# Second attention: score matmuls in pairs on two row tiles, with filler matmuls

## The chip, the core and the metric

The kernel is one program on one core of a Trainium2 chip. The metric is the device time of a whole execution in microseconds, the median of several runs.

## What is computed

The input is eight images of 256 x 256 and a text of 32 rows for each, together 288 tokens of 256 numbers for each image.

```python
def reference(x, txt, ...):
    h = tok(x)                          # wavelet split, gated details, synthesis
    h = concatenate([h, txt], axis=1)   # (8, 288, 256)
    h = h + L0_attn(layernorm(h))       # over the 8 images at one position
    h = h + L0_ffn(layernorm(h))        # 8 experts, top 2, and a shared one
    h = h + L1_attn(layernorm(h))       # the change is here
    h = h + L1_ffn(layernorm(h))        # 8 experts, top 2, and a shared one
    return h

def L1_attn(x, Wq, bq, Wk, bk, Wv, bv, Wo, bo):   # H, G, HD = 16, 4, 16
    q = (x @ Wq.T + bq).reshape(b, n, G, 4, HD)
    k = (x @ Wk.T + bk).reshape(b, n, G, HD)
    v = (x @ Wv.T + bv).reshape(b, n, G, HD)
    scores = einsum('bqghd,bkgd->bghqk', q, k) / sqrt(HD)
    y = einsum('bghqk,bkgd->bqghd', softmax(scores, -1), v).reshape(b, n, d)
    return y @ Wo.T + bo
```

So the second attention has, for each image, 16 query heads in 4 groups, each group with one key and one value head of 16 numbers.

## The kernel before, in words

The program holds the tokens in SBUF as `h`, 18 tiles of 128 rows (16 rows of each image in a tile). Six stages follow each other: the wavelet stage (to 52 us), the first attention (to 140), a layer norm with routing (to 159), the first experts (to 335), a layer norm and the second attention (to 611), and the output projection, routing and the second experts (to the end). Only the second attention changes.

Its numbers are float32 cut into a high and a low part (`split3` issues three matmuls for a product). For an image `i`:

- `project` makes q (two parts of 128 rows) and k, v (one part) for 288 positions, six matmuls for each of three parts `m`; DVE adds the bias (`qf`, L1135), ACT takes the high part (`qh`, L660), POOL the low part (`ql`, L457).
- SP writes `qh`, `ql` to DRAM (`stack_out`, L338) and reads them back (`stack_in`, L348, L351) as `QS` and `KS`: for each head the 16 numbers in rows 0 to 47, as high x high, high x low, low x high. Rows 48 to 95 are zero (`zeros`, L442). Rows 96 and 97 (`MROW`) hold the row maxima of the scores in `QS` and -1 in `KS`.
- Row scores (L1463, 36 for each image, 128 queries x 288 keys, banks 4 and 5 in turn) are made only for their maxima: DVE reduces each (L1125) into `MX`; after 18 of them PE transposes `MX` (L1510), DVE splits it into `Mh`, `Ml`, and SP sends it through DRAM into the rows 96 and 97 (`max_rows`, L358, L360).
- Transposed scores (L1481, 36 for each image, 96 keys x 384 queries, two at a time in banks 0 and 1 or 2 and 3) have K = 98: the product has the maximum taken off already. ACT takes the exponential of a pair of banks (L653) into the ring `PR`.
- Values (L1524): for each of 4 groups and 3 parts of keys, four matmuls, one for each head, into the four column tiles of bank 6. `VA` holds the values transposed (L1495) and a column of ones, which gives the sums. ACT copies each group out (`y_raw`, L707) and sends the sums through DRAM to be inverted and spread (L684 to L700; DVE L1148), and POOL multiplies (`divide`, L483, L486) into `yT`. The last image has its own way: PE spreads the sums (L1505), DVE inverts and multiplies (L1155 to L1163).

The work is one pipeline. `turn(it)` has `NU` = 18 steps `U`; turn `it` projects image `it`, makes the row scores of `it-1` (the first eight already in the turn before: `S_LEAD = 8`), the transposed scores of `it-2`, and the values of `it-2`, with the last in the turn of `it-3`. All engines run the same steps in the same order, written by the tables at the file's end:

```python
PR_U = [0, 1, 2]
VT_U = 3
MT_U = [5, 14]
SUM_U, SM_U, REC_U, RO_U, RB_U = [1, 2], 4, 7, 8, list(range(10, 18))
S_LEAD = 8
```

They give the steps of the projections, of the values' transposes, of the two transposes of the maxima, and of the sums' way. In one step PE issues two transposed scores, a row score, values if due, what the tables add, and a row score. Turns 4 to 7 are a loop. Behind the last turn come three `warm_up` matmuls and `out_project` (L1553).

Of the kernel before, what the change touches and what calls it, by code (L numbers as in the profile page):

```python
# [81 lines left out]
def build(nc, A, out):  # L82
# [156 lines left out]
    yr = [seq(f"yr{p}", [P, NGQ, POS], cur=k1) for p in range(2)]  # L239
# [3 lines left out]
    neg1 = at("neg1", [2, NGQ * POS], F32, k1[0])  # L243
# [60 lines left out]

    @block.sync
    def _(sp):
# [28 lines left out]
        def stack_out(i):

            sp.wait_ge(s["e_split"], 3 * (i + 1))
            sp.dma_start(scrH[ds(i, 1)].rearrange("o p m q -> (o p) m q"), qh[:, :, :].bitcast(F32)).then_inc(s["e_out"], 16)  # L338
            sp.dma_start(scrL[ds(i, 1)].rearrange("o p m q -> (o p) m q"), ql[:, :, :].bitcast(F32)).then_inc(s["e_out"], 16)

        def stack_in(i, p, m):

# [4 lines left out]
            for n, src in enumerate((scrH, scrH, scrL)):
                sp.dma_start(QS[p][n * HD:n * HD + HD, m * 8 * POS:(m + 1) * 8 * POS].bitcast(F32).rearrange("d (h q) -> d h q", h=8),  # L348
                             src[ds(i, 1), :, m, :].rearrange("o (h d) q -> d (o h) q", d=HD)).then_inc(s[f"e_in{m}"], 16)
            for n, src in enumerate((scrH, scrL, scrH)):  # L350
                sp.dma_start(KS[p][n * HD:n * HD + HD, m * 2 * POS:(m + 1) * 2 * POS].bitcast(F32).rearrange("d (g q) -> d g q", g=2),  # L351
                             src[ds(i, 1), m * 2 * HD:(m + 1) * 2 * HD, 2, :].rearrange("o (g d) q -> d (o g) q", d=HD)).then_inc(s[f"e_in{m}"], 16)

        def max_rows(i, p, b):
# [5 lines left out]
            sp.dma_start(QS[p][MROW:MROW + 2, b * NSH * P:(b + 1) * NSH * P].bitcast(F32),  # L360
                         scrM[ds(i, 1), :, b * NSH:(b + 1) * NSH].rearrange("o n c r -> (o n) (c r)")).then_inc(s[f"e_min{b}"], 16)

        def turn(it, p, pr, sp_, st):
            if pr:
                stack_out(it)
                if early(it):
                    stack_in(it, p, 0)
            if sp_:
                max_rows(it - 1, 1 - p, 0)
            if pr and not early(it):  # L370
                stack_in(it, p, 0)
            if sp_:
                max_rows(it - 1, 1 - p, 1)
            if pr:
                stack_in(it, p, 1)


        sp.wait_ge(s["e_const"], 3)
        turn(0, 0, True, False, False)
        sp.wait_ge(s["e_const"], 4)  # L380
        minus_ones(0)
        minus_ones(1)
        turn(1, 1, True, True, False)
        turn(2, 0, True, True, True)
        turn(3, 1, True, True, True)
        with sp.Fori(2, 4) as r:
            turn(2 * r, 0, True, True, True)
            turn(2 * r + 1, 1, True, True, True)
        turn(8, 0, False, True, True)
# [11 lines left out]
    def _(pool):  # L401
# [1314 lines left out]
```

## Time and profile before

| | |
|---|---|
| runs (3) | 848.50, 849.35, 849.79 us; median 849.35 |
| the profiled execution | 851.43 us, its span 849.6 us |
| granted TensorE clock, mean | 0.948 of 2.4 GHz |
| PE busy | 747.0 us (88%), 4842 matmuls |
| PEld (weight loads) | 632.8 us |
| DVE busy | 590.2 us (69%) |
| ACT busy | 340.3 us (40%) |
| POOL busy | 135.8 us (16%) |

The span goes from the first to the last instruction; the execution's own time is 1.8 us longer. PE is TensorE's matmuls and PEld its weight loads, which overlap them; DVE is VectorE, ACT is ScalarE, POOL is GpSimd, SP is SyncE, which issues DMAs. A granted clock of 1.00 is 2.4 GHz and 0.50 is 1.2 GHz. An engine's idle time matters only where it is on the way to the end.

### The profile page before, as it was taken

What the parts mean: (1) busy time and instruction counts of PE and PEld (TensorE: products, weight loads), DVE (VectorE), ACT (ScalarE), POOL (GpSimd) and SP (SyncE); (2) the same over time, 40 slices, a digit from 0 to 9 for tenths busy, and PEclk for the clock granted to TensorE, in tenths of its full rate; (3) what the DMA queues carried; (4) which work ended last, traced back from release to release, by engine and by line L of the source; (5) the groups of instructions that cost most, each with busy time, mean ns of one, the idle gap of its engine ahead of it and who ended that gap; (6) DMA issues with size and microseconds to landing.
All of it is one profiled execution on the core that took longest, in us unless ns stands there. A gap on an engine that the chain in (4) does not pass through costs nothing.

```text
span 849.6 us, 14457 instructions
## 1 busy us (share of the span) xinstructions
PE 747.0 (88%) x4842; PEld 632.8 (74%) x4842; DVE 590.2 (69%) x1357; ACT 340.3 (40%) x598; POOL 135.8 (16%) x128
## 2 busy tenths in 40 slices
PE   4639996899999998337999999999898999999997
PEld 3529994699999998226656556654476999999997
DVE  6295667677777777917676776773587777777776
ACT  1305443433333333200666666667434333333332
POOL 0105553000000000536113113311150000000000
PEclk9999996999999999556899999999999999999999
DMA  7210000000000000052434534430500000000000
GB/s 246 105 63 1 1 0 0 1 1 2 1 1 1 0 0 0 0 95 71 97 78 77 106 90 105 100 54 20 200 1 1 1 19 1 19 20 2 19 20 19
DMA packets 21559, 34.77 MB, mean 41 GB/s; under 512 B 6572, under 2 KB 17500, under 8 KB 20960
## 3 DMA queue, kind: packets, MB, share of 16 engines
q1 hardware_dynamic: 16632, 31.60, 13.9%
q10 hardware_dynamic: 4872, 2.46, 1.4%
q8 instruction: 32, 0.52, 0.3%
q14 instruction: 23, 0.19, 0.1%
HBM read 24.03 MB, written 9.99 MB: 40 GB/s over the span
## 4 chain that ended last, share of the span: by engine, by line
PE 78%; DVE 12%; ACT 3%; DMA 3%; issue 2%; SPq 1%; POOL 1%; ACTq 0%; DVEq 0%; POOLq 0%
PE PS L1222 17%; PE PS L1224 16%; PE PS L1223 16%; PE PS L1524 6%; PE PS L1463 6%; PE PS L1481 5%; DVE MX L1125 2%; PE PS L1553 2%; PE PS L1251 2%; PE PS L1230 1%; PE PS L1344 1%; PE PS L1310 1%; DMA KS<-scrH 1%; PE PS L1242 1%; DMA halves<-in_halves 1%
## 5 line engine op out<-in xcount | busy, mean ns | idle before, releaser
L1125 DVE TENSOR_REDUCE MX<-PS 128x1 f32<-128x288 f32 x288 | 125.1, 452 | 51.1 <-PE PS L1463 47.4
L1057 DVE SCALAR_TENSOR_TENSOR h<-PS,cmb,h 128x256 f32<-128x256 f32 (+1 forms) x342 | 143.9, 477 | 0.2 <-PE PS L1224 0.2
L653 ACT ACTIVATE PR<-PS 96x768 f32<-96x768 f32 x144 | 115.3, 806 | 47.3 <-PE PS L1481 44.9
L621 ACT ACTIVATE sg<-PS 128x384 f32<-128x384 f32 x114 | 55.8, 489 | 165.3 <-PE PS L1224 165.3
L1463 PE MATMUL PS<-KS,QS 96*128 96x288 f32 x288 | 97.9, 359 | 17.2 <-DMA KS<-scrH 14.9
L1042 DVE TENSOR_TENSOR al<-aa,ah 128x384 fp32r<-128x384 f32 x114 | 63.7, 558 | 67.0 <-ACT ah L625 67.0
L1463 PEld LDWEIGHTS PS<-KS,QS 96*128 96x128 f32 x288 | 57.2, 203 | 59.7 <-DVE MX L1125 40.3
L625 ACT ACTIVATE ah<-aa 128x384 fp32r<-128x384 f32 x114 | 59.9, 525 | 83.6 <-DVE aa L1036 83.6
L1222 PE MATMUL PS<-xTh,W1h 128*128 128x384 f32 x240 | 81.1, 338 | 0.0
L1036 DVE TENSOR_TENSOR aa<-sg,PS 128x384 f32<-128x384 f32 x114 | 63.3, 555 | 25.6 <-ACT sg L621 25.1
L1224 PE MATMUL PS<-xTl,W1h 128*128 128x384 f32 x240 | 80.9, 337 | 0.0
L1223 PE MATMUL PS<-xTh,W1l 128*128 128x384 f32 x240 | 80.9, 337 | 0.0
L1481 PE MATMUL PS<-QS,KS 128*96 128x384 f32 x288 | 75.7, 347 | 1.8 <-DVE MX L1125 1.0
L1222 PE MATMUL PS<-xTh,W0h 128*128 (+1 forms) x216 | 73.1, 338 | 0.0
L1224 PE MATMUL PS<-xTl,W0h 128*128 (+1 forms) x216 | 73.1, 338 | 0.0
L1223 PE MATMUL PS<-xTh,W0l 128*128 (+1 forms) x216 | 73.0, 338 | 0.0
L1524 PE MATMUL PS<-PR,VA 128*32 128x288 f32 x768 | 66.3, 418 | 1.1 <-ACT yr L707 1.0
L1222 PE MATMUL PS<-W1h,ah 128*128 128x256 f32 x180 | 51.1, 284 | 4.0 <-DVE al L1042 4.0
L1224 PE MATMUL PS<-W1l,ah 128*128 128x256 f32 x180 | 50.8, 282 | 0.0
L1223 PE MATMUL PS<-W1h,al 128*128 128x256 f32 x180 | 50.3, 279 | 0.0
L1222 PE MATMUL PS<-W0h,ah 128*128 128x256 f32 x162 | 46.0, 284 | 4.4 <-DVE al L1042 4.4
L1481 PEld LDWEIGHTS PS<-QS,KS 128*96 128x96 f32 x288 | 42.2, 165 | 9.5 <-ACT PR L653 4.5
(234 smaller groups left out, 1543.7 us busy)
## 6 DMA issues: line engine op xcount, KB each, us to landing
QS<-scrH SPq DMA_DIRECT2D x32, 144.0 KB, 3.8
W1raw<-in_w SPq DMA_DIRECT2D x1, 3840.0 KB, 11.5
W0raw<-in_w SPq DMA_DIRECT2D x1, 3456.0 KB, 10.6
scrH<-qh SPq DMA_DIRECT2D x8, 432.0 KB, 2.5
scrL<-ql SPq DMA_DIRECT2D x8, 432.0 KB, 3.2
QS<-scrL SPq DMA_DIRECT2D x16, 144.0 KB, 4.4
out_tokens<-h SPq DMA_DIRECT2D x6, 384.0 KB, 2.3
x_in<-in_x SPq DMA_DIRECT2D x2, 1024.0 KB, 6.5
```

What stands on the lines that cost most here:

```text
L625: A_(ah[:, b], aa[:, b], ACT.Copy).then_inc(s[f"f{L}_ah"], 1)
L653: A_(PR[0:KT, c0:c0 + 2, :], PS[0:KT, b:b + 2, 0:CW], ACT.Exp).then_inc(s["e_exp"], 1)
L1036: V.tensor_tensor(aa[:, b], sg[:, b], PS[:, 2 + b, 0:GW], ALU.mult).then_inc(s[f"f{L}_mul"], 1)
L1042: V.tensor_tensor(al[:, b], aa[:, b], ah[:, b].bitcast(F32), ALU.subtract).then_inc(s[f"f{L}_al"], 1)
L1057: ins = V.scalar_tensor_tensor(out=hj, in0=PS[:, b + t // 2, (t % 2) * D:(t % 2) * D + D], scalar=cmb[:, ds(g * GT + t, 1), e:e + 1].squee ...
L1125: V.tensor_reduce(MX[:, c // NSH, c % NSH:c % NSH + 1], PS[:, max_bank(it, c), 0:POS], AX_X, ALU.max).then_inc(s["e_mx"], 1)
L1222: M(out_, wh, xh, start=(start and c == 0), stop=False)
L1223: M(out_, wl, xh, start=False, stop=False)
L1224: ins = M(out_, wh, xl, start=False, stop=(stop and c == n - 1))
L1463: M(PS[:, max_bank(it, c), 0:POS], QS[q][0:MROW, c * P:c * P + P], KS[q][0:MROW, c // 9 * POS:c // 9 * POS + POS], start=True, stop=True). ...
L1481: ins = M(PS[0:KT, n % 4, 0:CW], KS[p][:, g * POS + kt * KT:g * POS + kt * KT + KT], QS[p][:, g * HQ + cc * CW:g * HQ + cc * CW + CW], sta ...
L1524: ins = M(PS[32 * hh:32 * hh + 32, 6, 0:POS], VA[p][:, kt, g, :], PR[:, c0:c0 + 3, :].rearrange("p c w -> p (c w)")[:, hh * POS:hh * POS + ...
```

## The change

- Scores in pairs. Heads of groups 0 and 1 now stand in rows 0 to 47 of `QS`/`KS`, those of groups 2 and 3 in rows 64 to 111, with the maxima in rows 48, 49 and 112, 113. Each step issues one pair of transposed scores (`scores`) and one pair of row scores (`row_scores`), the two of a pair on the row tiles at 0 and 64 and into two banks. Nothing is zero filled.
- DVE reduces both banks of a pair in one instruction. From turn 2 on all row-score pairs use banks 4 and 5, and each waits for the reduce before.
- `keep_busy`: two matmuls of 384 columns with no use, ahead of each projection (of images 2 to 7), values' transpose and maxima's transpose; and two at each step of turn 1 and of turn 2 up to step 8.
- Images 0 and 1 are projected ahead of the turns, then 16 `warm_up` matmuls; image `it+1` is projected in turn `it`. Row scores lag (`S_LEAD = -2`): image `it-1` from step 2 on, its last two in the next turn. Three buffers of `QS`, `KS` and `yr`. Values follow `AV_U`, in steps that have no projection; the second half of an image's values is in the next turn.
- The maxima's way is cut in two calls and has two reads; the inverses are read back a turn later (`RB_U`), those of image 6 in one piece behind turn 9. Half of image 0's stack is read by ACT's queue. The output bias is added in turns 3 to 5. No loops are left.

```diff
-MROW = 96
+TILE, MROW = 64, 48
-    QS = [seq(f"QS{p}", [P, NGQ * HQ], F32R, cur=k1) for p in range(2)]
+    QS = [seq(f"QS{p}", [P, NGQ // 2 * HQ], F32R, cur=k1) for p in range(NQB)]
...
+        for it in range(1, IMGS + 2):
+            if live(it, 0) and it > 1:
                 stack_out(it)
+            if live(it, 2):
+                max_out(it - 2, 1)
+                max_in(it - 2, 1)
+            if live(it, 0) and it > 1:
+                for a in range(2):
+                    stack_in(sp, it, a)
+            if live(it, 1):
+                max_out(it - 1, 0)
+                max_in(it - 1, 0)
...
+                if live(it, 4) and not last_image(it - 4) and U in RB_U and it < IMGS + 2:
+                    inverses_in(it - 4, RB_U.index(U))
+            if it == IMGS + 1:
+                for n in range(len(RB_U)):
+                    inverses_in(IMGS - 2, n)
...
-                    V.tensor_reduce(MX[:, c // NSH, c % NSH:c % NSH + 1], PS[:, max_bank(it, c), 0:POS], AX_X, ALU.max).then_inc(s["e_mx"], 1)
+                    V.tensor_reduce(MX[:, hf, z:z + NSH // 2 + 1:NSH // 2], PS[:, b:b + 2, 0:POS], AX_X, ALU.max).then_inc(s["e_mx"], 1)
...
+        def keep_busy(n, bank=6):
+
+            for _ in range(n):
+                M(PS[:, bank, 0:GW], xTh[:, 0, 0:P], xTh[:, 1, 0:GW], start=True, stop=True)
...
+        def scores(i, U):
+
+            g, kt, cc = U // 9, U % 9 // 3, U % 3
+            for a in range(2):
+                r = slice(TILE * a, TILE * a + MROW + 2)
+                ins = M(PS[0:KT, 2 * (U % 2) + a, 0:CW], KS[i % NQB][r, g * POS + kt * KT:g * POS + kt * KT + KT],
+                        QS[i % NQB][r, g * HQ + cc * CW:g * HQ + cc * CW + CW], start=True, stop=True, tile_position=(TILE * a, 0))
+            ins.then_inc(s["e_st"], 1)
+
+        def row_scores(i, c, bank):
+
+            g = c // (NSH // 2)
+            for a in range(2):
+                r = slice(TILE * a, TILE * a + MROW)
+                ins = M(PS[:, bank + a, 0:POS], QS[i % NQB][r, c * P:c * P + P], KS[i % NQB][r, g * POS:g * POS + POS],
+                        start=True, stop=True, tile_position=(TILE * a, 0))
+            ins.then_inc(s["e_s"], 1)
...
+                keep_busy(busy_at(it, U))
...
-                    wait(pe, s["e_mx"], NS * i + c - (3 if early(it) else 1))
+                    wait(pe, s["e_mx"], NSH * i + c - (1 if early(it) else 0))
+                    row_scores(i, c, max_bank(it, c))
...
+                if U in PR_U and live(it, -1) and it > 0:
+                    project(it + 1, PR_U.index(U))
...
+        for m in range(6):
+            project(m // 3, m % 3)
+        pe.wait_ge(s["e_prev"], 6)
+        warm_up(WARM)
+        last[0] = ("e_prev", 6)
+        for it in range(1, IMGS + 3):
+            turn(it)
...
-PR_U = [0, 1, 2]
-VT_U = 3
-MT_U = [5, 14]
+PR_U = [7, 12, 16]
+VT_U = 8
+MT_U = [11, 3]
-SUM_U, SM_U, REC_U, RO_U, RB_U = [1, 2], 4, 7, 8, list(range(10, 18))
+SUM_U, SM_U, REC_U, RO_U, RB_U = [9, 10], 14, 16, 17, list(range(4, 12))
-S_LEAD = 8
+S_LEAD = -2
+WARM = 16
+AV_U = [9, 10, 11, 13, 14, 15, 18, 19, 20, 22, 23, 24]
...
+def busy_at(it, U):
+
+    return 2 if it == 1 or (it == 2 and U < AV_U[0]) else 0
```

PE's order in the middle of turn 2 before: L1463 row scores, L1481 transposed scores, L1524 values, L1510 the transpose of the maxima.

```order
L1463 MATMUL PS<-KS_141,QS_139 128x288
L1524 MATMUL PS<-PR,VA_143 32x288 x4
L1463 MATMUL PS<-KS_141,QS_139 128x288
L1481 MATMUL PS<-QS_138,KS_140 96x384 x2
L1463 MATMUL PS<-KS_141,QS_139 128x288
L1524 MATMUL PS<-PR,VA_143 32x288 x4
L1463 MATMUL PS<-KS_141,QS_139 128x288
L1481 MATMUL PS<-QS_138,KS_140 96x384 x2
L1463 MATMUL PS<-KS_140,QS_138 128x288
L1510 MATMUL PS<-ident,MX 128x128
```

PE's order now, about steps 2 to 5 of a middle turn: L1452 a pair of transposed scores, L1461 a pair of row scores, L1477 values, L1428 fillers, L1533 the transpose of the maxima.

```order
L1461 MATMUL PS<-KS_142,QS_139 128x288 x2
L1477 MATMUL PS<-PR,VA_145 32x288 x4
L1452 MATMUL PS<-QS_138,KS_141 96x384 x2
L1461 MATMUL PS<-KS_142,QS_139 128x288 x2
L1428 MATMUL PS<-xTh 128x384 x2
L1533 MATMUL PS<-ident,MX 128x128
L1452 MATMUL PS<-QS_138,KS_141 96x384 x2
L1461 MATMUL PS<-KS_142,QS_139 128x288 x2
L1477 MATMUL PS<-PR,VA_145 32x288 x4
```

The number of score matmuls is the same; the row scores of a step stand together behind the transposed ones, and the fillers stand in a step without values.

ACT's order at the end of the turns before (L700 reads of the inverses of image 6, L653 exponentials, L707 copies of image 7's values):

```order
L700 DMA recb<-scrR 16x2x288
L653 ACTIVATE PR<-PS 96x768 [waits e_avt,e_st]
L707 ACTIVATE yr_154<-PS 128x288 [waits e_y,e_avt]
L700 DMA recb<-scrR 16x2x288
L653 ACTIVATE PR<-PS 96x768 [waits e_avt,e_st]
L700 DMA recb<-scrR 16x2x288
L653 ACTIVATE PR<-PS 96x768 [waits e_avt,e_st]
L700 DMA recb<-scrR 16x2x288
L707 ACTIVATE yr_154<-PS 128x288 [waits e_avt]
L718 ACT_TABLE_LOAD
```

And now (L666 exponentials, L684 the write of the inverses, L698 the reads, L704 the copies):

```order
L666 ACTIVATE PR<-PS 96x2x384 [waits e_st] x2
L684 DMA scrR<-rec 128x36 [waits e_rec]
L698 DMA recb<-scrR 16x2x288 [waits e_yt,e_ro]
L698 DMA recb<-scrR 16x2x288 x7
L704 ACTIVATE yr_156<-PS 128x288 [waits e_y,e_avt] x2
L715 ACT_TABLE_LOAD
```

The write and all eight reads of image 6 stand behind the last exponential and ahead of the last two copies.

## Rows read from the trace of the kernel before

**Rows 1.** The page, part 4: the chain that ended last, by engine.
```profile
PE 78%; DVE 12%; ACT 3%; DMA 3%; issue 2%; SPq 1%; POOL 1%; ACTq 0%; DVEq 0%; POOLq 0%
```
**Rows 2.** Stretch: length, busy us of PE, PEld, DVE, ACT, POOL, clock, DMA, GB/s.
```profile
456.00:482.00 26.00, 25.59 (x192) 15.44 (x191) 18.48 (x45) 17.04 (x29) 6.49 (x6) 1.00 0.45 94
```
**Rows 3.** Timeline of PE, transposed scores at turns' ends: start, length, instruction.
```profile
404.21 0.93 PE L1481 MATMUL PS<-QS,KS 128*96 128x384 f32 x2 [1.05 <-DVE MX L1125]
...
560.62 0.56 PE L1481 MATMUL PS<-QS,KS 128*96 128x384 f32 x2
...
582.49 0.95 PE L1481 MATMUL PS<-QS,KS 128*96 128x384 f32 x4
...
601.10 0.58 PE L1481 MATMUL PS<-QS,KS 128*96 128x384 f32 x2
```
**Rows 4.** Timeline of PE, one step with values.
```profile
497.93 0.51 PE L1481 MATMUL PS<-QS,KS 128*96 128x384 f32 x2
498.28 0.29 PE L1463 MATMUL PS<-KS,QS 96*128 96x288 f32 x1
498.50 0.69 PE L1524 MATMUL PS<-PR,VA 128*32 128x288 f32 x8
499.13 0.40 PE L1463 MATMUL PS<-KS,QS 96*128 96x288 f32 x1
499.37 0.51 PE L1481 MATMUL PS<-QS,KS 128*96 128x384 f32 x2
```
**Rows 5.** Timeline of PE, a projection's six matmuls; chain, six transposes.
```profile
510.11 0.40 PE L1222 MATMUL PS<-xTh,a1h 128*128 x1
...
511.03 0.30 PE L1463 MATMUL PS<-KS,QS 96*128 96x288 f32 x1
...
640.15 0.66 PE PS L1344 x6
```
**Rows 6.** Weight loads and matmuls of one L1524 group: ns min/median/max, first and last start.
```profile
L1524 PEld LDWEIGHTS PS<-PR,VA x8: 106/108/109, 498.5 to 498.6; 128*32 128x32 f32 x8
L1524 PE MATMUL PS<-PR,VA x8: 406/418/430, 498.5 to 498.8; 128*32 128x288 f32 x8
...
498.50 0.14 PEld L1524 LDWEIGHTS PS<-PR,VA 128*32 128x32 f32 x6 [0.21 <-issue]
```
**Rows 7.** DVE: reduces of row scores; the page's group; a reduce of 1152 elements.
```profile
499.57 1.89 DVE L1125 TENSOR_REDUCE MX<-PS 128x1 f32<-128x288 f32 x4 [0.50 <-PE PS L1463]
...
L1125 DVE TENSOR_REDUCE MX<-PS 128x1 f32<-128x288 f32 x288 | 125.1, 452 | 51.1 <-PE PS L1463 47.4
...
654.43 1.35 DVE L991 TENSOR_REDUCE t<-ra 128x144 f32<-128x1152 f32 x1
```
**Rows 8.** The page, part 5: ACT's exponentials.
```profile
L653 ACT ACTIVATE PR<-PS 96x768 f32<-96x768 f32 x144 | 115.3, 806 | 47.3 <-PE PS L1481 44.9
```
**Rows 9.** Head: PE's timeline, and stretches as in rows 2.
```profile
380.02 3.22 PE L1463 MATMUL PS<-KS,QS 96*128 96x288 f32 x9 [12.54 <-DMA KS<-scrH]
...
400.21 0.41 PE L1510 MATMUL PS<-ident,MX 128*128 128x128 f32 x1
...
381.00:382.00 1.00, 1.00 (x5) 0.68 (x3) 1.00 (x4) 0.00 (x0) 0.00 (x0) 0.50 1.03 110
...
388.00:392.00 4.00, 2.72 (x17) 2.04 (x15) 3.28 (x9) 0.89 (x4) 2.90 (x5) 0.96 0.19 75
...
396.00:400.00 4.00, 1.67 (x6) 1.12 (x5) 2.27 (x7) 0.00 (x0) 4.00 (x7) 0.50 0.69 85
```
**Rows 10.** Tail: DMA issues on ACT's queue, DVE's timeline, an issue group to landing.
```profile
595.74 0.83 ACTq L700 DMA_DIRECT2D recb<-scrR  x2
...
604.19 2.31 DVE L1158 SCALAR_TENSOR_TENSOR qf<-yr,halves,qf 128x288 f32<-128x288 f32 x1
...
610.40 0.46 DVE L1163 TENSOR_TENSOR yT<-qf,qf 128x288 f32<-128x288 f32 x1
...
scrR<-rec ACTq DMA_DIRECT2D x7, 18.0 KB, 2.1
```
**Rows 11.** Stretch in turn 9, columns as in rows 2.
```profile
594.00:597.00 3.00, 3.00 (x25) 1.44 (x24) 1.28 (x2) 2.38 (x4) 0.00 (x0) 1.00 0.09 25
```

More of the change, by code:

```diff
@@ L238, in build @@
     xn1 = at("xn1", [P, 2, GT, D], F32, k1[0])
[L239 removed]
+    yr = [seq(f"yr{p}", [P, NGQ, POS], cur=k1) for p in range(3)]
     SW = NGQ * HPG * POS // P
@@ L359, in max_rows, with max_in @@
+        def max_in(i, b):
             sp.wait_ge(s["e_mout"], 32 * (2 * i + b + 1))
[L360 to L364, printed above, removed]
-                stack_out(it)
[L366 to L375, printed above, removed]
@@ L378, in _ @@
[L378 to L389, printed above, removed]
+            for a in range(2):
+                r, c = TILE * a + MROW, b * NSH + a * (NSH // 2)
+                sp.dma_start(QS[i % NQB][r:r + 2, b * HQ:(b + 1) * HQ].bitcast(F32),
+                             scrM[i, :, c:c + NSH // 2].rearrange("n c r -> n (c r)")).then_inc(s[f"e_min{b}"], 16)
@@ L487, in divide @@
                                         recb[:, 2 * q + 1, :].rearrange("p (j c) -> p j c", j=NT), ALU.add).then_inc(s["e_yt"], 1)
[L489 to L498 removed]
+        for it in range(1, IMGS + 3):
+            if live(it, -1):
+                low_halves(it + 1)
+            if live(it, 4) and not last_image(it - 4):
+                divide(it - 4)
+            if 3 <= it < 6:
+                for j in range((it - 3) * NG, (it - 2) * NG):
+                    nc.gpsimd.tensor_tensor(h[:, j, :], h[:, j, :], bo1[:, :], ALU.add).then_inc(s["e_bo"], 1)
         pool.wait_ge(s["e_yl"], NGQ + 2)
@@ L717, in _ @@
+        for m in range(3):
+            high_part(0, m)
+        stack_in(act, 0, 1)
+        for m in range(3):
+            high_part(1, m)
+        for it in range(1, IMGS + 3):
+            turn(it)
         n1 = sum(WCOLS[1]) // NG
@@ L1531, in _ @@
         pe.wait_ge(s["e_hi"], NG)
-        for it in range(4):
-            turn(it, it % 2)
-        with pe.Fori(2, 4) as r:
-            last[0] = ("e_msplit", 2 * (2 * r - 1))
-            turn(2 * r, 0)
-            turn(2 * r + 1, 1)
-        last[0] = ("e_msplit", 14)
-        for it in range(8, 11):
-            turn(it, it % 2)
+        for m in range(6):
+            project(m // 3, m % 3)
+        pe.wait_ge(s["e_prev"], 6)
+        warm_up(WARM)
+        last[0] = ("e_prev", 6)
+        for it in range(1, IMGS + 3):
+            turn(it)
         warm_up(3)
```

386 lines of the change are left out of this document (185 added, 201 removed).

## The prediction

> **What bounds the kernel now.** I read the page's chain of waits first: 78% of it is TensorE (PE) [rows 1]. Then the stretches. In 456 to 482 us, the middle of the second attention, PE is busy 25.59 of 26 us at the full granted clock, DVE 18.48 and ACT 17.04 [rows 2]. So PE's own order sets the pace there. Then the timeline, for one step U (0 to 17 in a turn). Transposed scores (L1481) run from 404.21 (turn 2) over 560.62 (turn 8) and 582.9 (turn 9, the second pair of the four that begin at 582.49) to 601.10: six turns of 26.07, one of 22.3 with no projections and few row scores, and 18.2, 196.9 in all [rows 3]. All this is against the profiled execution, 851.43 us; the median of the runs is 849.35, that is 2.1 lower.
>
> One step with values, in PE's order [rows 4]: the scores L1481 at 497.93, the row score L1463 at 498.28, the values L1524 at 498.50, the next L1463 at 499.13, L1481 at 499.37. So two transposed scores take 0.35, values 0.62, a row score 0.22 ahead of values and 0.24 behind them, 1.43 in all. A matmul of 288 columns with no change of tiling ahead takes 0.137 (six of the projection from 510.11 to 511.03, less 0.10 for the change ahead of them [rows 5]). So a change into or out of column tiling costs about 0.10.
>
> **The change, part by part.**
> *Score pairs.* Per image 36 + 36 score matmuls of K = 98 and 96 become 18 + 18 pairs on two row tiles, 0-63 and 64-127. No row shows a row tile. The bounds: above, the pair costs as two (0.35 + 0.27); below, as one (0.175 + 0.137). The nearest rows are the column tiles of the values: eight weight loads of 108 ns each start within 50 ns [rows 6], and eight matmuls of 418 ns end 0.69 us after the first begins [rows 4]. Loads and matmuls of different tiles overlap there. I take the lower end and add 0.01 to 0.02 for the stagger.
> For each change between column tiles, row tiles and the whole array I charge the 0.10 that the rows show for column tiles.
>
> *The row-score loop.* Before, a row score waits for the maximum two back, in two banks. Now a pair fills both banks 4 and 5 and waits for the maximum of the pair just before it. One round: weight load to the start of DVE 0.44 (499.13 to 499.57 [rows 4, 7]); a reduce over 2 x 288 in place of 288, 0.45 + 288 x 1.04 ns = 0.75 (1152 elements take 1.35, 288 take 0.45 [rows 7], so 1.04 ns an element); release, by the gap between DVE's end and PE's start, 0.03. That is 1.22, and 1.33 if the second tile's load stands in line behind the first (0.11, the pitch of the transposes [rows 5]). PE's own work in a step with values: row pair up to the values 0.33 (its load is exposed), values 0.62, scores 0.28: 1.23. So the step takes 1.25, from 1.23 to 1.43 (nothing overlaps).
>
> *A full turn.* 11 steps with values at 1.25 = 13.75. Step 11 adds the maxima's transpose with its fillers (0.33 + 0.62 + 0.45 + 0.1 + 0.28): 1.77. The three projections: 0.33 + fillers (0.10 + 2 x 0.175) + six matmuls 0.82 + scores 0.28 = 1.88 each, 5.64. Step 8 (0.33 + 0.45 + three transposes 0.3 + 0.28) 1.35. Steps 3 and 17 at 1.25, the fillers of step 3 hidden in the loop. Waits for bank 7 at steps 8 and 12, 0.2. Sum 25.2. The twelve fillers are in it with 6 x 0.45 = 2.7, of which some 0.8 hides in the loop at steps 3 and 8. Without projections 23.3 (turns 7 and 8). Turn 9 is set by ACT: 18 x 0.80 for the exponentials [rows 8] and 4 x 0.41 for the copies = 16.1, I take 17.
> Turns 2 to 9: 5 x 25.2 + 2 x 23.3 + 17 = 189.6 against 196.9, **-7.3**.
>
> *Head.* The projections of both images now come first; image 0's end when they did, so its DMAs start when they did. Before, the first half of the stack releases PE at 380.02; now a pair needs both halves, and DMA is saturated to 382 (share 1.03 in its last microsecond [rows 9]). A second queue doesn't change the bytes, so 382. The zero fills of QS and KS go; they ended long before, so nothing. The larger fill of PR follows POOL's low halves of image 1; values need it some 25 us later, so nothing. What goes is the wait for image 1's stack, between 396 and 400, where PE is busy 1.67 of 4 us [rows 9]. Turn 1 is 16 steps: warm 0.77 each (fillers 0.45, pair 0.32), at 1.2 GHz about 1.4. With five at the low clock 7 + 8.5, three projections 3.6, transposes 1: 20. Turn 2 begins at 402 in place of 404.2: **-2**. Bounds: 399 (never cold) and 412 (all cold).
>
> *Tail.* ACT's order changes: the eight reads of image 6's inverses, which lay between exponentials, now stand ahead of image 7's last two copies of values. From the last scores T: the write of the inverses at T + 0.6, landed after 2.1, eight issues at 0.41 (two take 0.83) = 3.3, so the copy at T + 6 [rows 10]. Then three values 1.9, copy 0.5, and two chains of spread, reciprocal 1.96, product 0.52, sum 0.46, one after the other: the end at about T + 14.8, with one product stretched from 0.52 to 2.31, as at 604.19. Before: 610.86 - 601.10 = T + 9.8 [rows 3, 10]. **+5**. The second layer's weights are loaded once those reads have landed, 7 us ahead of the output projection where it was 7.4: nothing.
>
> *Queues and waits.* SP's order: the maxima's round trip. Before it took 4.0 us (transpose 400.21 to scores 404.21 [rows 3, 9]) and was given 13 steps; now it goes from step 11 to the next turn's step 0 and from step 3 to step 9, some 9.5 and 7.3 us, with two reads in place of one (+0.3) and, for the first half, some 2 us behind the stack's reads on SP's queue. It fits by 3 us, so nothing; if the reads of the inverses on ACT's queue slow it by more, PE waits (rival 3). POOL's additions of the bias move to turns 3 to 5, behind its low halves: nobody waits.
> Sum: -7.3 - 2 + 5 = -4.3: 847.1 profiled, **845.0** in the median.
>
> **The rivals.**
> 1. *The pair does not overlap, or row tiling drains longer than column tiling.* Then each step costs more. 104 steps (13 in each of seven turns, step 8, and three more in turns 7 and 8) carry it, so 10 ns a step is 1.04 us, and the point where the change turns slower is 41 ns a step. With the second load in line (1.33): -4.3 + 0.09 x 104 = +5, 854. With no overlap at all 11 steps at 1.43, 1.97, 3 x 2.08, 1.55, 2 x 1.37 and 0.2, a turn of 28.4: +3.2 in seven turns, 867. For it: no row tile in the trace; against: rows 6. The drain as a mechanism of this kernel: if each change had to wait for a matmul's flight beyond its own start, 0.30 - 0.14 = 0.16 [rows 5], in place of the 0.10 charged, twice a step, that is 0.12 x 104 = 12.5 us, 857.
> The Trainium skill (TensorEngine Tiling, Key Properties) has this as a rule: changing the tiling mode drains the engine. For column tiles the trace shows 0.10, less than the flight. The Trainium skill (TensorE: Matmul & The Clock Gate, Part 3) speaks for the overlap: matmuls on different row groups start some 4 ns apart; no row here shows it for row groups.
> 2. *The granted clock falls.* Before, turn 1 ran a row score (0.14 at the full clock) each 0.36 us: the clock, 0.96 at 388 to 392, was 0.50, which is 1.2 GHz, at 396 to 400 [rows 9]. In turn 9, where values and scores fill (12 x 0.62 + 18 x 0.35)/18.2 = three quarters, it stayed at 1.00, which is 2.4 GHz [rows 11]. A new step with values fills 0.62 + 0.18 + 0.14 of 1.25, three quarters too; steps 16 and 17 less. Each step at 1.2 GHz costs about 1 us. 2 of them a turn: +14, 859; one turn's worth in all, +18, 863.
> 3. *The maxima come late.* Each late half adds its lateness, once or twice a turn: 1 us each in seven turns is +14 at most, likely +5: 850.
> 4. *More gain:* the loop at 1.20, a warm turn 1, and a tail of +3: 839.
> 5. *It doesn't do what it says:* the built order shows pairs and fillers where they should be; whether the hardware overlaps them is rival 1.
>
> **How the numbers follow.** Forecast (overlap, clock up) 0.45, from 840 to 849; rival 4 0.10; rival 1 0.20 (the load in line 0.10, the drain 0.05, no overlap 0.05); rival 2 0.17; rival 3 0.08. The range takes in rival 4 and all but the ends of 1 and 2: 838 to 864. Within 0.2% (1.7 us, what a measurement can tell from no change) lie the upper edge of the forecast (0.05) and parts of rivals 1 and 3 (0.05): 0.10. Faster: 0.40 + 0.10 + 0.02 from rival 3 = 0.52. Slower 0.38.
>
> **What would show it.** Right: steps of 1.25 us, DVE's reduce on 576 elements at 0.75, PE waiting for it in steps with values; the pair's two matmuls starting within 0.03; turns of 25.2 and 23.3; first scores at 402; output projection some 15 us behind the last scores; clock 1.00 through turns 3 to 8. Wrong: pair matmuls 0.1 or more apart or the next step's start later than the reduce's end (rival 1), granted clock below 0.95 in turns 2 to 8 (rival 2), PE waiting for DMA QS<-scrM (rival 3).

## The result, and the profile after

The changed kernel takes 852.59 us in the median of 5 runs (850.86 to 854.15), the kernel before 849.35 (848.50 to 850.16). The ratio is 1.0039, 95% interval [1.0024, 1.0054]: **slower by 0.4%**, where 845.0 and "faster" were forecast. The intervals here leave out runs more than 1.5% above a kernel's fastest; where that matters below, all runs are given. The profiled execution of the change took 851.09 us (span 849.3), 0.3 less than the profiled one of before, 851.43; the balance below is made between these two.

One step with values, PE's timeline of the changed kernel (start, length, instruction), which answers to [rows 4]:

```profile
406.51 0.42 PE L1452 MATMUL PS<-QS,KS 50*96 50x384 f32 x2
406.82 0.40 PE L1461 MATMUL PS<-KS,QS 48*128 48x288 f32 x2
407.15 0.69 PE L1477 MATMUL PS<-PR,VA 128*32 128x288 f32 x8
407.77 0.41 PE L1452 MATMUL PS<-QS,KS 50*96 50x384 f32 x2
```

The step takes 1.26, and a pair of transposed scores 0.42 where two of them one behind the other took 0.51. The pairs overlap. DVE's group, from the page, which answers to [rows 7]:

```profile
L1128 DVE TENSOR_REDUCE MX<-PS 128x2 f32<-128x576 f32 x144 | 108.9, 757 | 68.8 <-PE PS L1461 67.6
```

The first transposed scores of turns 2 to 9 (step 0 of each), and the last (the lines between are left out), which answer to [rows 3]:

```profile
392.79 0.41 PE L1452 MATMUL PS<-QS,KS 50*96 50x384 f32 x2 [0.41 <-DVE MX L1128]
...
417.78 0.34 PE L1452 MATMUL PS<-QS,KS 50*96 50x384 f32 x2
...
443.35 0.33 PE L1452 MATMUL PS<-QS,KS 50*96 50x384 f32 x2
...
470.23 0.34 PE L1452 MATMUL PS<-QS,KS 50*96 50x384 f32 x2
...
496.01 0.34 PE L1452 MATMUL PS<-QS,KS 50*96 50x384 f32 x2
...
521.75 0.34 PE L1452 MATMUL PS<-QS,KS 50*96 50x384 f32 x2
...
545.20 0.34 PE L1452 MATMUL PS<-QS,KS 50*96 50x384 f32 x2
...
568.49 0.34 PE L1452 MATMUL PS<-QS,KS 50*96 50x384 f32 x2
...
594.05 0.76 PE L1452 MATMUL PS<-QS,KS 50*96 50x384 f32 x4
```

So the turns last 25.0, 25.6, 26.9, 25.8, 25.7 with projections, then 23.5, 23.3 and 25.9 (to the second of the last two pairs, 594.41): 201.6 against 196.9 before. The odd ones are the 26.9 and above all the 25.9 of turn 9, where 17 was forecast; there the granted clock is low. Stretches of the changed kernel (length, busy us of PE, PEld, DVE, ACT, POOL, clock, DMA, GB/s):

```profile
420.00:440.00 20.00, 19.57 (x165) 10.01 (x163) 12.52 (x20) 13.33 (x22) 1.60 (x2) 1.00 0.53 106
...
446.00:450.00 4.00, 4.00 (x27) 1.45 (x26) 1.58 (x3) 2.17 (x4) 3.55 (x6) 0.57 0.55 221
...
560.00:566.00 6.00, 5.31 (x47) 2.45 (x47) 3.67 (x7) 3.62 (x6) 3.75 (x3) 1.00 0.11 27
566.00:570.00 4.00, 2.64 (x22) 1.15 (x20) 2.56 (x4) 3.35 (x5) 0.44 (x1) 0.89 0.04 7
570.00:590.00 20.00, 19.32 (x113) 5.83 (x111) 2.08 (x4) 11.13 (x16) 1.02 (x1) 0.50 0.06 18
590.00:594.00 4.00, 4.00 (x26) 1.25 (x22) 2.33 (x2) 1.64 (x3) 3.16 (x3) 0.63 0.05 9
```

From 570 to 590 PE is busy 19.32 of 20 us and runs at 1.2 GHz all the while, where turn 9 of the kernel before stayed at 1.00 [rows 11]. Ahead of the two falls PE had pauses, in which it waited for the reduce of the maxima: it was busy 2.64 of 4 us from 566 on, and 3.15 of 4 from 442 on. A like stretch, 541 to 545 with 3.32 of 4, was followed by no fall. At the low clock a step of turn 9 looks like this, 1.68 instead of 0.9 to 1.0:

```profile
571.97 1.19 PE L1477 MATMUL PS<-PR,VA 128*32 128x288 f32 x8
573.09 0.63 PE L1452 MATMUL PS<-QS,KS 50*96 50x384 f32 x2
573.65 1.19 PE L1477 MATMUL PS<-PR,VA 128*32 128x288 f32 x8
```

The head went the other way. In the kernel before, DVE's small operations stood beside POOL's zero fills. POOL's timeline of the kernel before:

```profile
342.21 3.93 POOL L443 MEMSET QS<- 128x4608 f32 x1
346.09 1.05 POOL L444 MEMSET KS<- 128x1152 f32 x1
347.29 3.94 POOL L443 MEMSET QS<- 128x4608 f32 x1 [0.15 <-POOL KS L444]
```

DVE's of the same kernel:

```profile
342.40 4.77 DVE L748 TENSOR_SCALAR mv<-mt 128x3 f32<-128x3 f32 x1
...
347.42 3.83 DVE L753 TENSOR_SCALAR mt<-mv 128x3 f32<-128x3 f32 x1
```

and the same two operations in the changed kernel, where those fills are gone (L745 and L750 are L748 and L753 of before):

```profile
341.83 0.17 DVE L745 TENSOR_SCALAR mv<-mt 128x3 f32<-128x3 f32 x1
...
342.29 0.17 DVE L750 TENSOR_SCALAR mt<-mv 128x3 f32<-128x3 f32 x1
```

An operation on 128x3 elements took 4.77 us and ended at 347.17, when the fills of QS and KS end (346.09 + 1.05 = 347.14); the next took 3.83 and ended at 351.25, with the second fill of QS (347.29 + 3.94 = 351.23). This is what the Trainium skill (SBUF — State Buffer, Who interferes with whom) describes: GpSimd and some VectorE forms share a pair of ports, and the later one is blocked for the whole instruction. The chain of waits runs through these two operations, so the projections began at 362.82 before and at 354.27 now, 8.5 us earlier. From there to the first scores it is 38.5 us against 41.4: 2.9 more. The head gives 11.4.

The tail, in the changed kernel's chain of waits (start, length, what); it answers to [rows 10]:

```profile
594.87 1.46 DMA scrR<-rec
...
596.35 0.33 ACTq L698
600.10 0.42 ACT yr L704
...
603.14 1.97 DVE qf L1150
...
606.18 1.30 PE PS L1528 x2
607.47 3.27 PE PS L1223 x6
610.75 15.69 PE PS L1558 x72
```

The output projection (L1558) starts 16.3 us behind the last scores, 9.8 before: +6.5. Balance: -11.4 + 4.7 + 6.5 = -0.2, and the profiled executions differ by -0.3.

### The profile page after: what moved, and what is told of

Same layout as the page of the kernel before. It is cut to its first block, busy times and chain, and to the rows that moved or that the text cites. A ratio compares the mean times of both kernels' runs of the same rounds, so it can differ in the third digit from the quotient of the medians.

```text
span 849.3 us, 13715 instructions
## 1 busy us (share of the span) xinstructions
PE 762.6 (90%) x5012; PEld 619.7 (73%) x5012; DVE 566.2 (67%) x1213; ACT 341.0 (40%) x598; POOL 130.3 (15%) x124
## 4 chain that ended last, share of the span: by engine, by line
PE 81%; DVE 10%; DMA 2%; issue 2%; ACT 2%; SPq 1%; POOL 1%; ACTq 0%; DVEq 0%; POOLq 0%
PE PS L1215 16%; PE PS L1217 16%; PE PS L1216 16%; PE PS L1477 7%; PE PS L1452 5%; PE PS L1461 4%; PE PS L1428 4%; PE PS L1558 2%; PE PS L1244 2%; PE PS L1223 1%; PE PS L1337 1%; DVE MX L1128 1%; PE PS L1303 1%; PE PS L1235 1%; DMA KS<-scrH 1%
## 5 line engine op out<-in xcount | busy, mean ns | idle before, releaser
L1128 DVE TENSOR_REDUCE MX<-PS 128x2 f32<-128x576 f32 x144 | 108.9, 757 | 68.8 <-PE PS L1461 67.6
L666 ACT ACTIVATE PR<-PS 96x768 f32<-96x768 f32 x144 | 115.2, 806 | 62.8 <-PE PS L1452 62.1
L1033 DVE TENSOR_TENSOR aa<-sg,PS 128x384 f32<-128x384 f32 x114 | 63.2, 554 | 25.8 <-ACT sg L608 25.2
L1477 PE MATMUL PS<-PR,VA 128*32 128x288 f32 x768 | 73.7, 462 | 3.6 <-ACT yr L704 3.6
L1452 PEld LDWEIGHTS PS<-QS,KS 50*96 50x96 f32 x288 | 24.1, 165 | 55.5 <-issue 29.4
L1461 PE MATMUL PS<-KS,QS 48*128 48x288 f32 x288 | 54.5, 374 | 10.0 <-DVE MX L1128 9.5
L1452 PE MATMUL PS<-QS,KS 50*96 50x384 f32 x288 | 61.5, 428 | 1.1 <-ACT PR L666 0.7
L1461 PEld LDWEIGHTS PS<-KS,QS 48*128 48x128 f32 x288 | 27.7, 187 | 30.3 <-DVE MX L1128 15.0
```

The source lines that it names most:

```text
L666: A_(PR[0:KT, ca:cb + 1:cb - ca, :], PS[0:KT, b:b + 2, 0:CW], ACT.Exp).then_inc(s["e_exp"], 1)
L1033: V.tensor_tensor(aa[:, b], sg[:, b], PS[:, 2 + b, 0:GW], ALU.mult).then_inc(s[f"f{L}_mul"], 1)
L1128: V.tensor_reduce(MX[:, hf, z:z + NSH // 2 + 1:NSH // 2], PS[:, b:b + 2, 0:POS], AX_X, ALU.max).then_inc(s["e_mx"], 1)
L1452: ins = M(PS[0:KT, 2 * (U % 2) + a, 0:CW], KS[i % NQB][r, g * POS + kt * KT:g * POS + kt * KT + KT], QS[i % NQB][r, g * HQ + cc * CW:g * H ...
L1461: ins = M(PS[:, bank + a, 0:POS], QS[i % NQB][r, c * P:c * P + P], KS[i % NQB][r, g * POS:g * POS + POS], start=True, stop=True, tile_posi ...
L1477: ins = M(PS[32 * hh:32 * hh + 32, 6, 0:POS], VA[i % 2][:, kt, Y_G[n], :], PR[:, c0:c0 + 3, :].rearrange("p c w -> p (c w)")[:, hh * POS:h ...
```

## The experiments

The theory on record with the first seven: the clock falls because row-tiled pairs and column-tiled values hold it less than matmuls on the whole array; the zero fills slowed DVE; the tail is the eight issues on ACT.

**Without the fillers.** The two `keep_busy` calls at the transposes and the one in `project` go:

```diff
-                keep_busy(2, 7)
...
-                    keep_busy(2, 7)
...
-                    keep_busy(2, 7)
```

> The changed kernel without its 84 filler matmuls ahead of the projections and transposes. They are 12 of 0.22 us in a full turn, 2.6 us. Rival (fillers only cost): six full turns give back up to 2.6 each, 838 to 845. Theory (they hold the clock): the granted clock falls in turns 2 to 7 too, where a step with values takes 1.7 to 1.9 instead of 1.25; if half of the turns run so, 6 x 9 steps x 0.55 = 30 less 15, so 860 to 870.

Measured: 837.55 us (832.64 to 843.72, 6 runs), ratio to before 0.9844 [0.9820, 0.9868], 15.0 less than the changed kernel. **The rival was right**: the fillers only cost. (They have 384 columns and take 0.18 each at the full clock; the 512 columns and 0.22 of my expectations were wrong.) The transposed scores of step 17 in three turns with projections:

```profile
438.36 0.41 PE L1451 MATMUL PS<-QS,KS 50*96 50x384 f32 x2
...
462.33 0.41 PE L1451 MATMUL PS<-QS,KS 50*96 50x384 f32 x2
...
486.26 0.42 PE L1451 MATMUL PS<-QS,KS 50*96 50x384 f32 x2
```

24.0 a turn, 1.8 less than with fillers, and at the full clock. With 1.1 of turn 1 and the low stretch of turn 4 this kernel is 11.1 us ahead at the start of turn 7 (510.68 for 521.75); the rest of the 15.0 lies behind it, where the clock differs from run to run. The clock falls only from turn 7 on (stretches of this kernel):

```profile
456.00:482.00 26.00, 24.42 (x209) 12.17 (x209) 17.74 (x29) 17.94 (x30) 10.68 (x12) 1.00 0.59 105
520.00:540.00 20.00, 17.65 (x112) 7.02 (x108) 10.17 (x16) 11.26 (x19) 4.19 (x3) 0.60 0.49 72
540.00:560.00 20.00, 18.32 (x153) 7.37 (x145) 11.97 (x19) 12.46 (x21) 3.31 (x2) 0.89 0.09 22
```

From turn 7 on there are no projections. So my statement that fillers hold the clock in turns 2 to 7 falls for 2 to 6, and what the clock does in the last three turns is what sets the spread: the six runs go from 832.6 at a mean clock of 0.973 to 843.7 at 0.947.

**More fillers where it fell.** `keep_busy(more_at(it, U), 2 * (U % 2))` ahead of `scores`, with

```diff
+def more_at(it, U):
+    if it < 3:
+        return 0
+    return 2 if U == 17 or (it > IMGS - 2 and U in PR_U) or (it == IMGS + 1 and U in (MT_U[1], VT_U)) else 0
```

> The changed kernel with filler matmuls (full 128x128x512, two each time) also ahead of score pairs in stretches where the granted clock fell to 0.5 to 0.67 (446 to 450, 566 to 592): one place at the end of each turn from 3 on, three more in turns 7 to 9, two more in turn 9. Some 30 more fillers of 0.22 us are at most 7 us of TensorE time. Theory (the clock falls because the column-tiled value matmuls and row-tiled pairs do not hold it, and full-array matmuls do): the clock stays at 1.00 from 566 to 592, whose steps take 1.25 again instead of 1.7 to 1.9, some 10 us back after the fillers' own time, so about 842. Rival (fillers only cost time, the clock follows something else): the clock falls as before and the time is 855 to 860.

Measured: 845.06 us (844.42 to 860.57, 12 runs), ratio 0.9961 [0.9940, 0.9982]. As the theory had it: some 7.5 less than the changed kernel although PE has more to do. In the profiled execution the clock is 1.00 from 380 to 590. Ten of twelve runs lie between 844.4 and 847.9 with a clock of 0.966 to 0.975; two had a lower one (0.959 and 0.950) and took 854.6 and 860.6. The additional matmuls make the fall rarer; they don't exclude it. Whether they do it by their rows or by filling time is not shown: with them PE is busy 5.72 of 6 us from 566 to 572, where the changed kernel had the pauses, and the fillers on half of the rows, next, were not put at these places.

**Fillers on half of the rows**, same length and so the same busy share:

```diff
-                M(PS[:, bank, 0:GW], xTh[:, 0, 0:P], xTh[:, 1, 0:GW], start=True, stop=True)
+                M(PS[:, bank, 0:GW], xTh[0:TILE, 0, 0:P], xTh[0:TILE, 1, 0:GW], start=True, stop=True, tile_position=(0, 0))
```

(for bank 7 alone).

> The changed kernel with its fillers on 64 of the 128 rows (one row tile) and of the same length, so that TensorE's busy share is the same. Rival (the pauses of the engine decide about the clock): same time and same clock as the changed kernel, 852.6 within 2. Theory (matmuls on part of the array hold the clock less): the clock falls in more of the turns 2 to 7 and the time is at or above that without fillers, 860 to 880.

Measured: 852.88 us (850.90 to 858.40, 8 runs), clock 0.944 to 0.961. The median is the changed kernel's. The low clock begins one turn earlier in the profiled execution (0.66 at 540 to 566), but five of eight runs agree with the changed kernel's. This does not tell the two theories apart, and after the run without fillers one sees why: in turns 2 to 6 the fillers decide nothing.

**The rows of the scores, in the kernel before.** Its transposed scores run on all 128 rows (the `128*96` of [rows 4]), its row scores on 96, though only 50 and 48 of them carry data. Three kernels take rows away and leave the order, the number and the columns of the matmuls:

```diff
-MROW = 96
+MROW = 48
...
-        zeros(0)
-        zeros(1)
+        pool.sem_inc(s["e_const"], 2)
...
-                        ins = M(PS[0:KT, n % 4, 0:CW], KS[p][:, g * POS + kt * KT:g * POS + kt * KT + KT],
-                                QS[p][:, g * HQ + cc * CW:g * HQ + cc * CW + CW], start=True, stop=True)
+                        ins = M(PS[0:KT, n % 4, 0:CW], KS[p][0:MROW + 2, g * POS + kt * KT:g * POS + kt * KT + KT],
+                                QS[p][0:MROW + 2, g * HQ + cc * CW:g * HQ + cc * CW + CW], start=True, stop=True)
```

The two others have MROW = 66 and 62 and keep the zero fills.

> The kernel before, with its score matmuls on 50 rows instead of 98 and its row scores on 48 instead of 96, and therefore without the zero fills of QS and KS; no pairs side by side, no fillers. Theory for the start: the first projection comes at 354 instead of 362.8, 8.5 us of gain. Theory for the clock (matmuls on part of the array hold it less): the clock falls in more of turns 2 to 9 than before and takes some of the 8.5 back; if it does not, the time is 841.

> The kernel before with its transposed scores on 68 rows instead of 128 and its row scores on 66 instead of 96; zero fills kept, one matmul at a time as before, so only the number of rows differs from before, and no tile of 64 rows can be in play. Theory (the clock follows how much of the array the matmuls use): clock between the 0.82 of the version on 50 and 48 rows and the 0.95 of before, time between 870 and 940. Rival (a matmul of 64 rows or less is handled as a tile, and that makes the clock fall or the steps longer): clock and time as before, 850.

> The kernel before with its transposed scores on 64 rows and its row scores on 62, zero fills kept: only four rows fewer than the version on 68 and 66 (851.8, clock 0.942 to 0.949), fourteen more than the version on 50 and 48 (963, clock 0.79 to 0.83). If the clock follows the number of rows gradually: near the version on 68, 850 to 870. If what matters is whether a matmul reaches beyond 64 rows: near the version on 50, 930 to 975.

| rows, transposed / row scores | us, median (lowest to highest, runs) | clock, all runs |
|---|---|---|
| 128 / 96 (before, run beside each) | 848.8 to 850.4 (847.7 to 854.0) | 0.943 to 0.957 |
| 68 / 66 | 851.76 (849.87 to 854.87, 6) | 0.942 to 0.949 |
| 64 / 62 | 888.26 (874.74 to 915.15, 4) | 0.872 to 0.927 |
| 50 / 48 | 963.24 (945.67 to 975.48, 6) | 0.791 to 0.826 |

Stretches of the version on 50 and 48 rows, then of the one on 68 and 66, then of the one on 64 and 62:

```profile
400.00:440.00 40.00, 40.00 (x167) 23.27 (x168) 17.55 (x41) 16.49 (x27) 2.38 (x3) 0.50 0.17 40
440.00:460.00 20.00, 19.86 (x120) 11.90 (x119) 11.10 (x28) 10.32 (x19) 2.38 (x3) 0.80 0.37 88
...
476.00:482.00 6.00, 5.92 (x42) 3.55 (x40) 3.81 (x11) 4.00 (x9) 3.52 (x5) 1.00 0.23 86
482.00:500.00 18.00, 18.00 (x83) 9.48 (x82) 7.99 (x19) 7.91 (x11) 0.00 (x0) 0.50 0.30 66
```

```profile
503.00:520.00 17.00, 15.99 (x75) 9.66 (x74) 7.13 (x18) 6.05 (x10) 4.96 (x4) 0.60 0.29 48
520.00:560.00 40.00, 39.37 (x300) 23.73 (x298) 28.97 (x70) 27.12 (x46) 8.10 (x8) 1.00 0.46 100
```

```profile
440.00:457.00 17.00, 17.00 (x71) 10.36 (x72) 6.88 (x16) 5.69 (x8) 0.80 (x1) 0.50 0.22 36
...
480.00:560.00 80.00, 78.62 (x567) 46.23 (x564) 54.51 (x131) 50.11 (x84) 19.51 (x18) 1.00 0.42 90
```

On 50 and 48 rows PE is busy for 40 us without a pause and has 1.2 GHz, and at 482 the clock falls again though PE was busy 5.92 of the 6 us before. So here pauses of PE neither keep it low nor bring on this fall. Besides the rows only the zero fills were taken, and the version on 64 and 62 rows, which has them, loses the clock too. That rows matter in the kernel before is shown; by what law is not. The version on 64 and 62 shows something more: its clock stays low from the head of the attention to 457 and is 1.00 from there to the end of the scores, though the turns with projections are alike. So the same instructions ran for long at either level, and the four runs of this version spread over 40 us.

Of the expectations one had the size, the 850 that the rival gave for 68 and 66. On 50 and 48 rows the fall was to take back some of 8.5 us, and it cost over 110; the 888 on 64 and 62 lies between both forecasts. A time that follows the rows in proportion is excluded (128 to 68 costs 1.4 of 850, ratio 1.0014 [0.9993, 1.0034], and one low stretch in the profiled execution; 68 to 64 costs 36.5 in the medians). A mere boundary at 64 is not enough either, as 64 and 50 differ by 75.

The Trainium skill (TensorE: Matmul & The Clock Gate, Part 1) lets the clock depend on how busy the PE has been of late. Taken as the busy share of the profile, the trace of the version on 50 and 48 rows disagrees: 1.00 of busy time at a clock of 0.50.

The version on 50 rows also starts its projections at 353.83 instead of 362.82, 9.0 earlier, as expected without the fills.

**The fills put back** into the changed kernel, on POOL behind the fill of MX, with nobody using their result:

```diff
+        for p in (0, 1, 2, 0):
+            own(nc.gpsimd.memset(QS[p][:, :].bitcast(F32), 0.0))
+            own(nc.gpsimd.memset(KS[p][:, :].bitcast(F32), 0.0))
+            own.settle()
+        pool.sem_inc(s["e_const"], 1)
```

and the later waits for `e_const` one higher.

> The changed kernel with two zero fills of half-size QS and KS buffers twice over (the same 10 us of POOL's memsets as the kernel before has) put back behind the maxima's fill on POOL; nothing uses their result. Theory (POOL's fills stretched VectorE's small operations from 342 to 351): the first projection starts 8.5 us later again (362.8 instead of 354.3) and the time is about 861. Rival (the start came earlier for another reason, for example the order of waits): the first projection stays at 354 and the time at 852.6.

Measured: 859.62 us (857.26 to 864.25, 6 runs), ratio 1.0126 [1.0102, 1.0150], 7.0 more than the changed kernel; the first projection starts at 360.40, 6.1 later. The theory holds, with 6 to 7 in place of 8.5: these fills are half as long each and began 1.2 us earlier (341.02 for 342.21), and they met the two operations for 1.89 and 1.82 us instead of 4.77 and 3.83, and later three operations on 256 elements (3.77 for 1.05).

**The tail, with image 6's inverses on SP's queue**, alone and together with the additional fillers:

```diff
+        sp.wait_ge(s["e_ro"], 16 * (IMGS - 1))
+        sp.wait_ge(s["e_yt"], NGQ // 2 * (IMGS - 2))
+        for n in range(len(RB_U)):
+            hh, b = divmod(n, 2)
+            r = 32 * hh + HD * b
+            sp.dma_start(recb[r:r + HD, b::2, :], scrR[IMGS - 2, hh, b::2].unsqueeze(0).broadcast_to([HD, NGQ // 2, POS])).then_inc(s["e_rb"], 16)
...
-            if it == IMGS + 1:
-                for n in range(len(RB_U)):
-                    inverses_in(IMGS - 2, n)
```

> The changed kernel with the eight issues of image 6's inverses on SP's queue instead of ScalarE's, where they stood ahead of the copies of the last y. The trace of the changed kernel shows 3.65 us of them at 596.35 in the chain, and TensorE waiting 3.56 for the copy. Theory: 3.6 to 5 us less, 848 to 849. Rival (the end hangs on another chain that ends just as late, the division of image 6 on POOL): 851 to 853.

> The changed kernel with both the additional fillers and the last inverses on SP's queue. If the two losses are separate terms their gains add: about 842 less 4, so 838, which is faster than both kernels. If the additional fillers do nothing to the clock: 852 to 856.

Alone: 853.07 us (844.70 to 856.21, 12 runs), ratio 1.0013 [0.9987, 1.0039]; the clock went from 0.943 to 0.967 between its runs, and 11.5 us of spread hide a term of 4, so this run settles nothing. Together: 845.02 us (843.98 to 847.58, 5 runs), ratio 0.9934 [0.9915, 0.9953], against 845.06 with the fillers alone: **the gains don't add**. The two profiled executions show why. With both, the output projection starts at 603.74, 12.3 us behind the last scores, with the fillers alone at 607.02, 16.4 behind. (The clock has a part in this: from 596 to 605 it was low with the fillers alone and 1.00 with both.) What holds the output projection with both is the chain that the rival of the first of these two runs names, POOL's division of image 6: PE waits 2.28 for it. But the profiled spans are 845.8 and 845.6. DVE's timeline of the version with both:

```profile
619.58 0.96 DVE L1176 TENSOR_TENSOR h<-PS,h 128x768 f32<-128x768 f32 x1 [0.52 <-PE PS L1562]
620.57 1.08 DVE L837 BATCH_NORM_STATS2 stats<-h 128x6 f32<-128x256 f32 x3
621.69 0.23 DVE L744 TENSOR_TENSOR mt<-stats 128x18 f32<-128x18 f32 x1
621.84 2.92 DVE L745 TENSOR_TENSOR mt<-stats 128x18 f32<-128x18 f32 x1
624.68 0.18 DVE L746 TENSOR_TENSOR mt<-stats 128x18 f32<-128x18 f32 x1
```

and POOL's, the subtraction for the second layer's weights, which ends at 624.70:

```profile
613.20 11.50 POOL L498 TENSOR_TENSOR W1l<-W1raw,W1h 128x1280 fp32r<-128x1280 f32 x4 [9.52 <-ACT W1h L722]
```

An operation on 18 elements a row takes 2.92 and ends with POOL's. It is the same picture as with the zero fills. With fillers alone POOL is done at 622.97 and DVE comes to this place at 625: nothing collides. The weights' load waits for the reads of the inverses, so it came 1.1 us later (598.88 instead of 597.82), and 2.7 of the gain of 3.3 went in this one operation.

**Fillers only from turn 7 on**, with the tail on SP. The fillers of `project` go, those at the transposes stand under `FILL if it > IMGS - 2 else 0`, and

```diff
+def more_at(it, U):
+    if it < IMGS - 1:
+        return 0
+    return FILL if U == 17 or (it > IMGS - 2 and U in PR_U) or (it == IMGS + 1 and U in (MT_U[1], VT_U)) else 0
```

with FILL = 2, and then 1.

> The changed kernel with fillers only from turn 7 on, where no projections are left: two each at the additional places and at the transposes of turns 7 to 9; none in turns 2 to 6; the last inverses on SP's queue. Theory (in turns 2 to 6 the projections hold the clock and fillers only cost, from turn 7 on the clock falls without them): turns 2 to 6 take 23.9 as in the kernel without fillers, turns 7 to 9 keep 1.00 with 24.2, 24.5 and 19.0 as in the one with more fillers; 845.0 less 5 x 2.0, so 835. Rival (what holds the clock in turn 7 is the fillers of the turns ahead too): the clock falls in 6 or 7 as in the kernel without fillers, and the time is 838 to 845.

> The same with one filler at each place instead of two, 0.22 us less at some 17 places. If half as many full-array matmuls hold the clock: 835 less 3, so 832. If they don't: the clock falls in turns 7 to 9 in some runs and the time spreads from 832 to 842.

Measured with two: **835.69 us** (833.75 to 840.72, 5 runs), ratio 0.9828 [0.9801, 0.9855], 1.7% faster than before and 2.0% less than the changed kernel, and as the theory had it (835). Turns 2 to 6 take 23.3 to 24.0. Four of the five runs have a clock of 0.973 to 0.975 and take 833.8 to 836.2; the profiled one is the fifth, and lost some us:

```profile
535.00:550.00 15.00, 14.32 (x85) 5.30 (x84) 7.58 (x12) 7.33 (x10) 1.92 (x3) 0.57 0.06 12
```

With one: 842.75 us (830.53 to 850.65, 6 runs), two runs at 0.973 and 0.975 take 831.2 and 830.5, the four others, at 0.945 to 0.959, 842.7 to 850.7. One filler at each place is cheaper when the clock holds, and it held in two runs of six; so the second forecast, a spread, had the kind and not the size. Against the version with no fillers at all (837.55) the one with two is not told apart in the median; its runs spread over 7.0 us instead of 11.1.

## Why the prediction was wrong

**Score pairs and the loop: right.** "So the step takes 1.25": 1.26 measured, the reduce 757 ns for 0.75. In steps without values PE waits 0.68 for the reduce and the step is 1.25 as well; in those with values the weight load of the row pair starts 0.05 behind the reduce's end (408.07 for 408.02). So the loop sets both, as forecast. Rival 1 is out, the pair overlaps and changes of tiling cost no more than charged.

**Full turns: nearly.** "Sum 25.2": 25.6 to 25.8 at the full clock (the 26.9 has the low stretch at 446 to 450 in it), 25.0 in turn 2. The fillers' share, 2.7 less 0.8 hidden a turn, was right: taking them out gave 1.8. What I did not ask is whether anything was won by them there. Turns 7 and 8 took 23.5 and 23.3 where I had 23.3 for each. The five turns with projections are 129.0, forecast 126.0, and 1.2 of that is the clock: this part of the sum held to 2 us.

**Granted clock: the step that failed.** The forecast set turn 9 at 17, at the full clock. It took 25.9, nearly all of it at 1.2 GHz. In the version with both, at 1.00 from 560 to 600, turn 9 took 19.3 with 12 additional fillers of 0.18 in it, so some 17.1 without, which is an estimate. So the low clock cost about 25.9 - 17.1 = 8.8, and 1.2 more in turn 4 (26.9 for 25.7): **some 10 us** of the 12.0 by which turns 2 to 9 exceed the forecast. In the tail it cost 1.7 (1.19 for 0.69 in the last values, 1.27 and 1.30 for 0.68 in two spreads), where the kernel before had lost 0.5 in one spread (1.16). Rival 2 had the mechanism ("the granted clock falls", 0.17) and near enough the size (+14), but looked at steps 16 and 17 of full turns; it happened above all in turn 9, and there I had argued from how much of the time matmuls *fill* (three quarters before, three quarters after). The runs on fewer rows show that this quantity does not decide alone: with the same matmuls in number, order and columns the mean clock was 0.95 on 128 and 96 rows and 0.79 to 0.83 on 50 and 48. The text also gave the scores "K = 98"; the row says `128*96`, all rows of the array, and I read past it. What is shown is that the clock fell in turn 9, what it cost, and that additional matmuls there mostly bring it back. That the pairs lose it by their rows, as the kernel before does when its rows are taken, is argued and not shown; the pauses ahead of the fall are a rival that no run separates from it.

**Head: a second step that failed, by 9 us in the other direction.** "The zero fills of QS and KS ... ended long before, so nothing." They ended before their readers, and that was the wrong question. The chain of waits of before had the two operations of 4.77 and 3.83 us on 3 elements a row in it, and I did not look at that stretch. Even the rows had a case of it: the product stretched "from 0.52 to 2.31, as at 604.19" stood beside POOL's division (603.59 to 606.20), and in the changed kernel it took 0.91. Putting fills back costs 7.0. This also moved the row scores' start from 382 to 373.5. The rest of the head, "2", was 2.9: turn 1 never went cold and took 19.3 from the first row scores, for which I had 20.

**Tail: right in kind.** +5 forecast, +6.5 measured; the 1.7 of the low clock are in it. The terms as I named them give more than the T + 14.8 that I wrote: 6 + 1.9 + 0.5, twice 2.94, and 1.8 for the stretch are 16.1. Against that the 16.3 measured is near partly by luck, as the stretch was 0.4 and the low clock made up for it. "The second layer's weights ...: nothing" holds for the change, but they stand just behind it: when the tail was shortened by 3.3, DVE's wait behind POOL's subtraction of these weights took 2.7 of it.

**Maxima and queues: right.** PE waits nowhere for QS<-scrM. Rival 3 is out.

So the profiled -0.2 is -8.5 (fills, missed), -2.9 (rest of the head), +4.7 (turns: -7.3 forecast, so 12.0 off, of which the clock is some 10 and the full turns 1.8) and +6.5. In the medians the change is at +3.2, since the profiled execution of before was 2.1 above its median and that of after 1.5 below. Against the profiled -4.3 the errors are +12.0 (turns), +1.5 (tail) and -9.4 (head): two large ones of opposite sign, which nearly cancel. Where the clock falls varies from run to run and from version to version, so that one number for turns 7 to 9 had little basis; a chance for the low clock at least as high as that for the full one would have been the honest form.

What stays open: whether rows or pauses begin the low clock in turn 9; why 68 rows hold the clock nearly as 128 do and 64 don't; whether the values' column tiles have a part in it (no run changed them); and whether the low clock in turn 4 (446 to 450) and those in turns 7 to 9 begin by the same cause.

## What to carry to other kernels

Packing small matmuls side by side shortens the step, but ask first what then holds TensorE's clock: in the kernel before, rows that only multiply zeros had held it. Put fillers only where the trace shows a low clock, and try the kernel without any first: here taking 84 of them away gave 15 us, and those few that were placed in the last three turns kept the clock at 0.973 or more in four runs of five. And before a fill or a copy on GpSimd is called hidden, look at what VectorE does at that moment: an operation of 0.17 us on the critical chain can take as long as GpSimd's.

## What was not expected of the hardware

- TensorE at 1.2 GHz for 40 us with a busy share of 1.00 (version on 50 and 48 rows, 400 to 440). Same number of matmuls and columns on 128 and 96 rows: mean clock 0.95. On 64 and 62 rows one execution had both levels, 0.50 up to 457 and 1.00 from there to the end of the scores.
- Executions of one program differ by 1 to 2% along with the clock: 832.6 us at a clock of 0.973 and 843.7 at 0.947 (version with no fillers), 830.5 at 0.975 and 850.7 at 0.945 (one late filler at each place).
- A VectorE operation on 128x3 elements took 4.77 us beside GpSimd's fills, 0.17 without; one on 128x18 took 2.92 beside a GpSimd subtraction. Both ended within 0.1 us of GpSimd's end.
